# A decoder layer with experts: a GpSimd subtraction cut in quarters, and another order of GpSimd's work in the last attention batches

## The reference

```python
x = x + attention1(layernorm(x))                # one head, causal, with a position slope
x = x + attention2(layernorm(x), ctx, mask)     # 16 heads of 16 channels
x = x + experts(layernorm(x), w_gate, w_gate_up, w_down)

# experts: 8 of them, 2 for each token
p = softmax(x @ w_gate); keep the two largest of each token, scaled to the sum 1
g, u = split(x @ w_gate_up[e]); expert_out[e] = (silu(g) * u) @ w_down[e]
out = sum over the two experts of p[e] * expert_out[e]
```

## Time and profile before

| | |
|---|---|
| median of 3 runs | 1202.6 us (1196.9 to 1209.24) |
| profiled execution | 1195.79 us, of it span 1194.0 us |
| TensorE busy | 1083.6 us (91%) |
| VectorE busy | 705.1 us (59%) |
| ScalarE busy | 664.6 us (56%) |
| GpSimd busy | 502.2 us (42%) |
| mean granted clock of TensorE | 0.967 |

### The profile page before, as it was taken

The page is one execution under the profiler, slowest core; times in us unless marked ns, Lnnn a source line. Parts: engine busy times, 40 slices in busy tenths (PEclk is TensorE's granted clock), DMA queues, the critical chain, the costliest instruction groups (busy, mean ns, idle before and its releaser), DMA issues.

```text
span 1194.0 us, 37034 instructions
## 1 busy us (share of the span) xinstructions
PE 1083.6 (91%) x12828; PEld 898.4 (75%) x12828; DVE 705.1 (59%) x2156; ACT 664.6 (56%) x1446; POOL 502.2 (42%) x421
## 2 busy tenths in 40 slices
PE   5579889988999898997699999999999999999996
PEld 4456665656666565663488999999999999999996
DVE  5456778878777778777256444444444444444443
ACT  5467777878877776774534443344343444434442
POOL 5444655556655555542233432332323323323332
PEclk9889999999999998899899999999999999999998
DMA  7445555545566553424932344229312122128321
GB/s 226 150 139 160 141 140 150 159 121 159 163 157 165 159 144 116 122 81 150 329 92 33 43 133 140 33 36 388 92 31 35 28 33 35 28 34 276 102 36 19
DMA packets 91663, 142.66 MB, mean 119 GB/s; under 512 B 20960, under 2 KB 69536, under 8 KB 88288
## 3 DMA queue, kind: packets, MB, share of 16 engines
q1 hardware_dynamic: 75790, 122.95, 33.4%
q0 software_dynamic: 15808, 19.09, 9.9%
q10 hardware_dynamic: 18, 0.01, 0.0%
HBM read 268.13 MB, written 43.47 MB: 261 GB/s over the span
## 4 chain that ended last, share of the span: by engine, by line
PE 58%; DVE 17%; DMA 9%; issue 9%; SPq 3%; POOL 2%; ACT 1%; DVEq 0%; POOLq 0%; ACTq 0%
PE t_ring L1828 15%; PE front L1828 15%; PE pv L1846 7%; PE s_ring L1846 7%; DMA x_in<-in_x 6%; DVE nmax L1090 3%; DMA slot_entry<-entries 2%; PE s_ring L1613 2%; DVE xn L1035 2%; PE pv L1644 2%; DVE stats L1021 2%; PE front L1484 2%; SPq L402 2%; DVE gprob L1137 1%; PE front L1471 1%
## 5 line engine op out<-in xcount | busy, mean ns | idle before, releaser
L699 POOL DMA_INDIRECT out<-y_sb,place_i x71 | 111.9, 1576 | 320.9 <-DVE y_sb L1380 122.7
L1828 PE MATMUL front<-rows_hi,wgu_sb 128*128 128x128 f16 x2272 | 213.5, 219 | 0.0
L1828 PE MATMUL t_ring<-rows_hi,wgu_sb 128*128 128x128 f16 x2272 | 213.5, 219 | 0.0
L1090 DVE TENSOR_REDUCE nmax<-s_ring 128x2 f32<-128x512 f32 x256 | 165.9, 686 | 75.7 <-PE s_ring L1613 75.1
L1828 PE MATMUL front<-rows_lo,wgu_sb 128*128 128x128 f16 x1136 | 197.6, 219 | 0.0
L1828 PE MATMUL t_ring<-rows_lo,wgu_sb 128*128 128x128 f16 x1136 | 197.6, 219 | 0.0
L833 ACT ACTIVATE probs_t<-t_ring,mask_bias 128x512 f32<-128x512 f32 x256 | 168.5, 687 | 31.5 <-PE t_ring L1629 28.8
L1828 PEld LDWEIGHTS front<-rows_hi,wgu_sb 128*128 128x128 f16 x2272 | 180.5, 98 | 2.4 <-issue 0.8
L1828 PEld LDWEIGHTS t_ring<-rows_hi,wgu_sb 128*128 128x128 f16 x2272 | 180.6, 98 | 1.6
L1411 DVE SCALAR_TENSOR_TENSOR act_t<-t_ring,silu_g 128x256 f32<-128x256 f32 x142 | 60.2, 424 | 150.7 <-ACT silu_g L973 150.7
L973 ACT ACTIVATE silu_g<-t_ring 128x256 f32<-128x256 f32 x142 | 54.5, 384 | 166.0 <-PE t_ring L1828 166.0
(11 more groups left out here) (225 smaller groups left out, 2175.5 us busy)
## 6 DMA issues: line engine op xcount, KB each, us to landing
wgu_sb<-gu_split SPq DMA_DIRECT2D x71, 2048.0 KB
wd_sb<-down_split SPq DMA_DIRECT2D x71, 1024.0 KB
w_piece<-in_w_gu SPq DMA_DIRECT2D x32, 512.0 KB, 8.4
gu_split<-w_halves SPq DMA_DIRECT2D x32, 512.0 KB
w_piece<-in_w_down SPq DMA_DIRECT2D x16, 512.0 KB, 9.8
down_split<-w_halves SPq DMA_DIRECT2D x16, 512.0 KB
x_in<-in_x SPq DMA_DIRECT2D x16, 256.0 KB, 7.1
ctx_in<-in_ctx SPq DMA_DIRECT2D x16, 256.0 KB, 8.3
```

What stands on the lines that cost most here:

```text
L699: nc.gpsimd.indirect_dma_start(out=out, out_offset=bass.IndirectOffsetOnAxis(ap=place_i[:, j:j + 1], axis=0), in_=y_sb[:, j], in_offset=No ...
L1090: nc.vector.tensor_reduce(nmax[:, n // HJ, :, n % HJ], s_ring[n % 2][:].rearrange("p (r k) -> p r k", r=2), AX.X, ALU.max, negate=True).th ...
L1828: o = nc.tensor.matmul(gu_ring[f][:, part * SLOT:(part + 1) * SLOT], wgu_sb[j][:, w, at:at + P], r[:, j % 2, c], start=(i == 0), stop=(i = ...
```

## The change

`split_lo` subtracts a piece in four instructions of 256 columns, of which the last counts the piece; columns and values are the same. In the last batches VectorE converts the row numbers of slots 0 to 3 ahead of the gate of batch 13 where it did so after its placement. GpSimd's iteration 14 is written out: the output's low half and the square root of batch 13 stay first; the four gathers and the low half of batch 14 now come before the scatter of batch 13, and the square root of batch 14 after it.

```diff
+LOCKED = 256
...
             def split_lo(k, i):
                 pool.wait_ge(piece_hi, CHUNKS * k + i + 1)
-                nc.gpsimd.tensor_tensor(w_halves[:, i, 1], w_scaled[:, i], w_halves[:, i, 0], ALU.subtract
-                                        ).then_inc(piece_split, 1)
+                pool.sem_inc(pool_passed, 1)
+                for c in range(0, CHUNK, LOCKED):
+                    o = nc.gpsimd.tensor_tensor(w_halves[:, i, 1, c:c + LOCKED], w_scaled[:, i, c:c + LOCKED],
+                                                w_halves[:, i, 0, c:c + LOCKED], ALU.subtract)
+                o.then_inc(piece_split, 1)
...
-            iteration(14, 0, 7, True, True, True, False, False)
+            out_rest(B - 3)
+            rsqrt_tail(B - 3)
             for p in range(2):
                 pool.wait_ge(normed_out[p], 16 * ((EARLY_TOKENS + 1 - p) // 2 + 1))
             for j in range(STREAMS):
                 gather(j, j)
             out_rest(B - 2)
+            scatter(B - 3, 1, B // 2 - 1)
             rsqrt_tail(B - 2)
...
                 h_max(b + 1, 13, 16)
+                for j in range(STREAMS):
+                    slot_rows(j, j, 0)
                 t_choose(b - 1, 1)
                 t_place(b - 1, 1)
...
             last_maxima()
-            for j in range(STREAMS):
-                slot_rows(j, j, 0)
             last_attention()
```

## The result

The kernel after the change takes 1169.87 us in the median (1168.36 to 1170.65, 4 runs) against 1200.12 us (1196.9 to 1209.24, 4 runs): ratio 0.973, 95% interval 0.968 to 0.979. That is 30 us less; 21.3 us had been forecast.

What follows compares the result with a forecast made beforehand. Batches were bound by a ring of waits through VectorE, stalled by GpSimd pieces; expert slots by TensorE. Norm 16.0, gate 3.4, L1029 1.2 and order 0.7 summed to 21.3 us: 1202.6 to 1181.3 us, range 1161 to 1197.

Steps and rivals of the forecast that it cites:

- the ring: Attention batch: second norm, maxima, gate, query low half, stores, input fetch, back to VectorE; delaying VectorE there lengthens the batch.
- Quarters of 0.67 us, following each other by 0.63: GpSimd's piece subtraction: each 256-column instruction takes 0.67 us, the next follows after 0.63, a piece occupies 2.56 us.
- The norm is caught twice and ends 1.6 us after the piece's issue: VectorE's second norm: each half waits for a GpSimd quarter; 1.0 us gained per batch, 16.0 us in 16.
- rival A: Second norm and gate: both norm halves pass together, gate waits half a quarter; 38.5 us gained, 1164 us; chance 0.15.
- rival B: Second norm and gate: GpSimd keeps VectorE out through all four quarters; slower, 1214.8 us; chance 0.08.
- The gate gains 3.4 us: VectorE's gate: shorter waits beside pieces in five, five and three batches of different kinds; 3.4 us, between −4 and +13.
- The L1029 stall gains 1.2 us: VectorE's L1029: its one stall shrinks from 1.8 to at most 0.6 us, gaining 1.2 us.
- All of it passes: Attention batches: TensorE's 1.76 us norm wait exceeds the 1.0 taken, so stall gains count in full, 20.6 us.
- The step that failed: the clock: TensorE in the batches: no term in the sum; up to 1 us in some nine batches appeared only under a rival.
- rival C: Batches: another engine or fetch takes the place of VectorE's stalls, half passes; 11 us gained, 1191.6 us; chance 0.15.
- The order is worth 0.7 us: Last batches: TensorE's 5.68 us wait vanishes off the path; conversions cost 0.5, moved gathers gain 1.3; net 0.7 us.
- Rival D: Last batches: the 5.68 us count as well, if the crowded fetch lands 5 us sooner; 1176 us; chance 0.10.

Runs made afterwards that it cites:

- halves: The kernel after the change with two instructions of 512 columns a piece instead of four: 1186.21 us beside 1196.88 for the kernel before, ratio 0.992.
- fill: The kernel before with ten unused products added on TensorE in each batch ahead of its second-norm wait: 1180.02 us against 1194.72, ratio 0.987.
- quarters_only: The kernel before with only the four-instruction pieces, last batches in the old order: 1162.28 us beside 1196.88, ratio 0.972.
- order_only: The kernel after with the whole piece put back, leaving only the new order of the last batches: 1195.25 us beside 1196.88, ratio 0.998.
- late_rows: The kernel after with slot 4's row-number conversion moved to slot 1 and its gather behind the last batch's low half: 1156.07 us against 1194.72, ratio 0.968.
- guard_both: The kernel before, whole pieces; piece 1 waits for the second norm, piece 2 for the gate's one-hot rows: 1174.99 us against 1205.79, ratio 0.977.

## Why the prediction was right, and where it was not

The direction, the part that does it and the ring were right, the measured time lies in the range, and the gain was 30 us where 21.3 had been forecast. The time of 1181.3 us was 11.4 too long: 9 us are missing gain, and 2.5 come from the median it started from, 1202.6 us where the four runs give 1200.12. Point by point:

- **Quarters of 0.67 us, following each other by 0.63.** Measured 0.68 us and four in 2.56 to 2.66 us (301.81, 281.01). Right.
- **The norm is caught twice and ends 1.6 us after the piece's issue.** 281.38 + 1.13 − 281.01 = 1.50; 1.1 us gained in each batch, 17.6 us for 16.0. The halves (2.11 us) show the same rule at another length. Right; rival A's 0.7 us pair did not occur, and rival B (VectorE kept out) is refuted, and with it what I had drawn from the Trainium skill (GPSIMD Engine Reference, section 2.1): that the cores overlap in consecutive instructions does not keep VectorE out here.
- **The gate gains 3.4 us.** The excess went from 18.0 to 13.0 us, 5.0. The size holds, the picture half: the mixture of cases that I carried over vanished. In every batch L1143 now just precedes the piece, and L1153, L1155 and L1158 are caught, the case for which I had forecast a loss of 0.2 us. It costs 1.00 us where with a whole piece it cost 1.04, so the three batches that were of this kind before gain next to nothing, and not −0.2 us. The gain is that of the other ten, in which L1137 had been caught for 1.2 to 1.8 us.
- **The L1029 stall gains 1.2 us.** The longest one fell from 1.94 to 0.62 us, as said. But three were caught in the batches and not one, and over 60 to 530 us their excess went from 1.8 to 1.1 us: 0.7.
- **All of it passes.** It did. fill and quarters_only both run at clock 1.00, and from one to the other the batches lose 387.9 − 374.3 = 13.6 us, where 13.3 us went from twelve norms and 0.7 from the gate.
- **The step that failed: the clock.** The sum had no term for it. I had the row, a batch at 1.00 in 32.07 us and one at 0.95 in 33.08, named up to 1 us in some nine batches for the dips, and put them into rival A alone, as though TensorE had to lose its whole wait before they went. A wait of 1.75 us shortened to 0.65 was enough: no stretch at 1.2 GHz is left in the twelve batches. fill prices that at 9 to 13 us. The ledger of quarters_only's twelve batches says the same: of 27.1 us, norms make 13.3 and the gate 4.6, and 9.2 are left. With 9 us more the forecast would have been 30. That it would meet the measured number so well is partly luck: the other terms came out 2.7 us larger in sum, and late batches of the kernel after (see rival C) took some of it back. The regular batches took 30.9 us where 31.6 had been forecast. The ledger is one trace against one, and single late batches could shift it by several us; the price by regular batches does not hang on them, and fill's medians, 14.7 us apart, agree with 9 us and the gate's 4.
- **The order is worth 0.7 us.** order_only gives 0.2% with an interval of −0.5% to +0.1%: no more than that can be said, and it agrees. Its mechanism is shown by the traces and late_rows: TensorE's 5.68 us went, VectorE's wait grew to 6.59 us (8 forecast), TensorE's to 5.02, and a stretch of 6.8 us at 1.2 GHz stands there now and no longer at the old wait, which I had not forecast. Rival D's 5 us were met in number and not in cause. Counted from the last second norm the entries landed 5.4 us sooner, but 3.2 us of that is an earlier issue (at +43.4 instead of +46.6), and quarters_only, without the order, has 2.3 of it. The fetch itself took 2.2 us less, and most of what the order gained there was lost behind it.
- **Rival C** (another wait holds the ring) did not show on average. It did in single batches: one of the kernel after took 33.96 us (153.50 to 187.46), with a fetch of the input of 9.44 us behind a late SyncE queue. quarters_only has none like it. The 6.6 us between the two traces' twelve batches are such batches, and what makes them late is not settled; such batches, not the clock, part the two traces, which both stand at 1.00.

## What to carry to other kernels

Here, instructions of VectorE with two tiles in SBUF, and copies, casts and scalar operations there, took a multiple of their plain length and ended when a GpSimd instruction ended; the maxima and index searches of the gate beside the same pieces kept their plain 0.24 and 0.16 us (after, 285.85 and 286.31). It is worth looking for by comparing one line's minimum and maximum, and the cure is to make the GpSimd instruction short, or to let it begin only behind the VectorE instructions on the path. Count how often a run of VectorE instructions will be caught, not only how long each catch is: cutting in two helped little, since the norm was caught twice.

When a stall is taken from in front of TensorE, give the clock a term of its own: here it was worth half as much as the stalls themselves. And when a reorder frees an engine, look for the next wait on the freed path before counting the gain.

## What the runs showed of the hardware that I had not expected

- Ten products more a batch made the kernel 1.3% faster [0.8%, 1.7%]: 37.5 us at 1.2 GHz cost some 9 to 13 us (the clock, above).
- A VectorE instruction slips in ahead of a GpSimd instruction that was issued 0.02 us after it (before, 294.75 against 294.77), and one issued 0.04 us after (guard_both, 220.44 against 220.40) waits for the whole 2.13 us.
- A cast of four columns (L1155) is caught in the same way: 0.60 us beside quarters, 1.09 beside halves, for 0.17 plain.
- A GpSimd subtraction cost 434, 678, 1167 and 2132 ns for 128, 256, 512 and 1024 columns.
